# A graph-attention kernel on one core: the opening loads chained by waits instead of issued together

## The reference

```python
h = relu(layernorm(x))                      # x: 2048 x 256
type_sum = adj @ h                          # adj: 2048 x 2048 of 0 and 1, for both types
attn_a = sigmoid(concat([type_sum, h]) @ Wa.T + ba)
attn_b = sigmoid(concat([type_sum, h]) @ Wb.T + bb)
hw = h @ W_sa
scores = (hw @ a_left)[:, None] + (hw @ a_right)[None, :]
e = where(adj != 0, exp(-leaky_relu(scores, 0.01)), 0)
x_a = (e / (sum(e, axis=1) + 1e-5)) @ hw
x_b = adj @ (h @ W_gcnb) + b_gcnb
out = x + sigmoid(attn_a * x_a + attn_b * x_b)
```

## Time and profile before

| | |
|---|---|
| median of 3 runs | 190.69 us (190.56 to 190.69) |
| span of the profiled execution, first to last instruction | 189.2 us |
| total of the profiled execution | not given beside its span |
| TensorE matmul busy | 175.0 us, 92% |
| VectorE busy | 154.3 us, 82% |
| ScalarE busy | 117.3 us, 62% |
| GpSimd busy | 37.1 us, 20% |

### The profile page before, as it was taken

One profiled execution on the slowest core, in us unless ns is written; L12 is line 12 of the kernel. 1 busy time (PEld: TensorE's weight loads), 2 busy tenths in 40 slices (PEclk: granted clock), 3 DMA queues, 4 the chain that ended last, 5 costly groups with the idle time before them and its releaser, 6 DMA issues.

```text
span 189.2 us, 4431 instructions
## 1 busy us (share of the span) xinstructions
PE 175.0 (92%) x1576; PEld 144.4 (76%) x1576; DVE 154.3 (82%) x389; ACT 117.3 (62%) x231; POOL 37.1 (20%) x86
## 2 busy tenths in 40 slices
PE   0359899999999999999999999999999999999993
PEld 0335465466888888888888888888888888888892
DVE  0698789999999989996997898599869896997341
ACT  2197586899647958664696458466727764594310
POOL 1057770099970010002000200020020000000000
DMA  5920797000029008311901470175109210001100
GB/s 141 396 102 0 110 185 155 2 3 0 0 28 196 2 5 155 67 59 16 196 15 55 63 158 6 49 120 102 55 0 178 43 55 0 0 0 55 61 28 28
DMA packets 4621, 13.67 MB, mean 72 GB/s; under 512 B 512, under 2 KB 896, under 8 KB 4608
## 3 DMA queue, kind: packets, MB, share of 16 engines
q0 software_dynamic: 2304, 8.39, 24.8%
q1 hardware_dynamic: 2016, 4.20, 6.2%
q10 hardware_dynamic: 288, 0.92, 1.3%
HBM read 19.80 MB, written 2.10 MB: 116 GB/s over the span
## 4 chain that ended last, share of the span: by engine, by line
PE 80%; DVE 3%; issue 0%; ACT 0%; DVEq 0%
PE ps L800 15%; PE ps L801 15%; PE ps L807 14%; PE ps L808 14%; PE ps L806 14%; PE ps L765 4%; PE ps L838 1%; PE ps L837 1%; PE ps L836 1%; DVE mv_lo L603 1%; PE ps L756 1%; DVE h0t_lo L581 1%; DVE mv_lo L601 1%; PE ps L745 0%; DVE e_raw L342 0%; DVE far L333 0%
## 5 line engine op out<-in xcount | busy, mean ns | idle before, releaser
L349 ACT ACTIVATE e_raw<-e_raw,log_e 128x512 f32<-128x512 f32 x64 | 46.1, 720 | 43.9 <-DVE e_raw L342 43.1
L806 PE MATMUL ps<-mv_lo,e_hi 128*128 128x257 f16 x240 | 65.5, 273 | 0.0
L808 PE MATMUL ps<-mv_hi,e_lo 128*128 128x257 f16 x240 | 65.5, 273 | 0.0
L807 PE MATMUL ps<-mv_hi,e_hi 128*128 128x257 f16 x240 | 65.4, 272 | 0.0
L342 DVE SCALAR_TENSOR_TENSOR e_raw<-sl_row,exs,far 128x256 f32<-128x256 f16 (+1 forms) x128 | 56.6, 482 | 2.5 <-DVE far L333 2.0
L801 PE MATMUL ps<-mv_lo,adj 128*128 128x258 f16 x256 | 56.9, 272 | 0.0
L800 PE MATMUL ps<-mv_hi,adj 128*128 128x258 f16 x256 | 56.9, 273 | 0.0
L360 DVE TENSOR_TENSOR e_lo<-e_raw,e_hi 128x512 f16<-128x512 f32 x64 | 44.5, 697 | 3.8 <-ACT e_hi L356 3.8
L356 ACT ACTIVATE e_hi<-e_raw 128x512 f16<-128x512 f32 x64 | 39.3, 616 | 0.0
L800 PEld LDWEIGHTS ps<-mv_hi,adj 128*128 128x128 f16 x256 | 24.7, 96 | 3.8 <-ACT sl_row L471 0.2
L801 PEld LDWEIGHTS ps<-mv_lo,adj 128*128 128x128 f16 x256 | 24.8, 97 | 3.3
(11 more groups left out here) (80 smaller groups left out, 179.9 us busy)
## 6 DMA issues: line engine op xcount, KB each, us to landing
adj<-in_adj_t POOLq DMA_DIRECT2D x16, 512.0 KB, 7.1
x_sb<-in_x SPq DMA_DIRECT2D x4, 512.0 KB, 8.0
out<-res SPq DMA_DIRECT2D x7, 256.0 KB, 2.0
w_sb<-in_weights ACTq DMA_DIRECT2D x1, 512.0 KB, 8.1
c_sb<-in_consts ACTq DMA_DIRECT2D x1, 391.0 KB, 5.7
out<-res SPq DMA_DIRECT2D x1, 128.0 KB, 1.8
out<-res SPq DMA_DIRECT2D x2, 64.0 KB, 1.6
```

What stands on the lines that cost most here:

```text
L349: act.activation(e_raw[:, p % RING, :, :], e_raw[:, p % RING, :, :], ACT.Exp, bias=log_e[:, 0:1], scale=SLOPE - 1.0).then_inc(exp_done, 1)
L806: pe.matmul(a_bank(s, q), e_hi[:, j, cols], mv_lo[:, j, 0, 0:D + 1], start=(j == 0), stop=False)
L807: pe.matmul(a_bank(s, q), e_hi[:, j, cols], mv_hi[:, j, 0, 0:D + 1], start=False, stop=False)
L808: return pe.matmul(a_bank(s, q), e_lo[:, j, cols], mv_hi[:, j, 0, 0:D + 1], start=False, stop=(j == NT - 1))
```

## The change

SyncE now waits, before it issues each group of x but the first, until the group before has landed. ScalarE waits, before it issues consts and weights, until group 0 of x has landed. Nothing else is changed.

```diff
--- before.py
+++ after.py
@@ -228,6 +228,8 @@
         @block.sync
         def _(sp):
             for g in range(NG):
+                if g:
+                    sp.wait_ge(x_landed[g - 1], 16)
                 sp.dma_start(x_sb[:, g * GT:(g + 1) * GT, :], x[:, g * GT:(g + 1) * GT, :]).then_inc(x_landed[g], 16)
             with sp.Fori(0, NCH // 2 - 1) as r:
                 for s in range(2):
@@ -433,6 +435,7 @@
 
         @block.scalar
         def _(act):
+            act.wait_ge(x_landed[0], 16)
             act.dma_start(c_sb[:, :], consts).then_inc(c_landed, 16)
             act.dma_start(w_sb[:, :, :, :], weights).then_inc(w_landed, 16)
```

## The result

The kernel after takes 192.97 us (median of 4 runs, 192.81 to 193.21) against 190.69 us: ratio 1.0118, 95% interval 1.0106 to 1.0131, 2.28 us more. The forecast of 191.1 with a range up to 192.4 was wrong: the sign held, the size did not. The profiled execution took 192.81 us, with a span of 191.1 (before 189.2); the other three spans are 191.2 to 191.5, so it is the shortest of the four, and 1.9 us of the difference can be followed in it.

The account below looks back on a forecast made before the run. The prediction took the opening, up to the start of TensorE's adjacency and attention products, as the bound. Late consts move `relu_high(0)` from 12.03 to 12.5; 190.69 + 0.47 = 191.16, given as 191.1 us, range 190.0 to 192.4.

Parts of the forecast that it names:

- R: Start of `relu_high(0)` on ScalarE, 12.03 us before the change; forecast to move to 12.5 us.
- E: Start of the first `exs` on VectorE, 16.45 us before; forecast to move by 0.47 us, to 16.9.
- the idle spell before L451: Sign on ScalarE: idle time before this line, released by TensorE, the line starting at about 12.5 us.
- R = C + 3.9: Opening: `relu_high(0)` starts 3.9 us after consts land, behind `wl` and `turn(0)` on TensorE; 12.5 us forecast.
- Time = 190.69 + (C - 8.13): Kernel time for each rival, from the consts' landing time; a landing at 8.13 us is break-even.
- Part 2: Opening loads: consts issued behind group 0 at 4.56 land at 8.6 us instead of 6.56, the added cost.
- first touch of a new region: Opening of an adjacency load: the slow start isn't only sharing; first touch cost about 1 us there.
- Slower by much: Rival, opening loads: every fresh start is slow, consts again take 5.7 us; 192.8, half way 191.9; chance 0.13.
- No change: Rival, opening loads: x packets slow only from sharing, consts land between 7.75 and 8.5; centre 190.7 us; chance 0.25.
- Faster: Rival, opening loads: group 0 at full rate, consts land below 7.75; 189.9 us, at the middle 190.2; chance 0.15.
- The early transposes get quicker: Rival, TensorE's opening: gapless work speeds `turn(1)`, 190.8 us, or `turn(0)` itself, 190.3; chance 0.12.
- Parts 1 and 3: Opening loads: group 0 lands at 4.5 us, 1.85 earlier, table load hidden; weights and groups 1 to 3 hidden.

## Why the prediction went wrong

**The path was right.** What bounds the kernel, the fixed piece from R to E, TensorE taking over from ScalarE at R, the idle spell before L451 (now L454), `wl` and turn without a gap: all are in the profile after. R = C + 3.9 gives 14.0 for the measured C of 10.14, and R was 13.90; from R to E it was 4.44 us (4.42 before). Time = 190.69 + (C - 8.13) gives 192.7 for that C, and 192.97 was measured. Across the versions R, E and the time go together as long as group 1 of x is in time: R 11.19 with 189.90, 12.69 with 191.69, 13.04 with 191.87, 13.19 with 192.26, 13.90 with 192.97. The medians scatter about this by up to 0.4 us (with only ScalarE's wait R was 14.06 and the time 192.77); the spans don't: from E to the end of the span it was 172.7 to 172.8 us in all twelve profiled executions, the kernel before included. So nothing behind E took part in any of these differences.

**The step that failed is the sum for C** (C is the landing of the consts), in Part 2: "Consts land at C = 4.56 + 1.0 + 2.5 + 0.55 = 8.6 us." It was 10.14. Of the 1.54 us, about 0.4 is group 0's landing (4.97, not 4.5) and 1.1 the consts' own stage (5.2, not 4.05).

In the second, the failing term is the 2.5 us for "consts and group 1, interleaved": with the start of 1.0 and the tail of 0.55 left as they are, 3.6 were needed. It assumed that two queues that start together share the engines from the first packet and at full pace. ScalarE's queue gets next to nothing in its first microsecond beside SyncE's. The record had a sign of it that the prediction used only for a rival: before the change, too, consts were issued with group 0 at 0.86 and took 5.7 us, against 3.1 alone.

The prediction's reading that "c's packets took 163 ns from the first, so the slowness was x's" is wrong as well. The 163 ns are a mean over 5 us. In the first microsecond of data of the kernel before, ScalarE's queue showed, from 2.0 to 2.5 and from 2.5 to 3.0 us:

```profile
q10 hardware_dynamic: 5, 0.02, 22.4%
...
q10 hardware_dynamic: 5, 0.02, 10.8%
```

That is a mean of 266 ns for the consts' first ten packets (16.6% of 16 us), and in the next microsecond 157 (34 for 33.3%); SyncE's queue moved 32 packets meanwhile, then 36. Consts alone took 276 ns per packet in their first microsecond (45 for 77.6%). So the slow packets belong to the start and not to x, and the stage behind a wait pays for them again. Why they are slow no run shows, nor does any show the "first touch of a new region" to which the prediction put it down.

In the first, the data of group 0 alone took less per packet than I charged (193 ns, 38.6% of 64 us from 1 to 5 us for 128), but didn't end together. The windows from 2.5 to 4.5 us (engines' busy time, PEclk, DMA share, GB/s):

```profile
2.50:3.00 0.50, 0.00 (x0) 0.00 (x0) 0.00 (x0) 0.00 (x0) 0.00 (x0) 1.00 1.08 319
3.00:3.50 0.50, 0.00 (x0) 0.00 (x0) 0.00 (x0) 0.00 (x0) 0.00 (x0) 1.00 0.62 246
3.50:4.00 0.50, 0.00 (x0) 0.00 (x0) 0.00 (x0) 0.00 (x0) 0.00 (x0) 1.00 0.46 188
4.00:4.50 0.50, 0.00 (x0) 0.00 (x0) 0.00 (x0) 0.00 (x0) 0.00 (x0) 1.00 0.16 66
```

The engines are full for one half microsecond, and then their mean share falls to 0.62, 0.46 and 0.16 until the landing. The profile doesn't name single engines, but it shows 16 packets under 512 B, which I take for the ends of the load on the 16 engines (argued, not shown). Counted in half microseconds from 3.0 us on, they are 4, 6, 5 and 1. A mean per packet times 128 over 16 is too short for a load that ends so unevenly; 4.1 us for 512 KB alone is the right row.

**The rivals.** "Slower by much" is what happened, with a chance of 0.13: C = 10.2, 192.8. Its number was right partly by luck, as 4.5 + 5.7 has group 0 0.5 us too early and the stage 0.5 us too long. Its reason was half right: not every fresh start costs 5.7 us (consts alone took 3.1), but each start of consts on ScalarE's queue beside a load on SyncE's took 5.2 to 5.7. "No change" is out with C at 10.14. "Faster", by full-rate opening loads, is out: group 0 alone took 4.1 us. "The early transposes get quicker" is out too: `turn(0)`, directly behind `wl`, took 1.95 us for eight (2.08 before) and `turn(1)` 2.16 (2.17 before), far from the later 1.04. The granted clock reads 1.00, the level of 2.4 GHz, in every window of the opening, both where TensorE is slow and where it is fast, so this reading doesn't tell the two paces apart. Rather the slow pace lasted longer: the first products of `wide(0, 0)` took 0.63 us each up to 20.67, where before they took 0.38 from 17.39 on. It cost nothing, as E and the chain behind it don't wait for them: from E to the first adjacency product it was 28.54 us, before 28.49.

The Trainium skill's sum (DMA: Bandwidth & Descriptors, Anatomy of one DMA), which the page fits to transfers issued by GpSimd, gives as estimates 2.0 + 0.9 = 2.9 us for the consts alone, 2.0 + 1.2 = 3.2 for group 0 alone, and 4.1 for consts and group 1 together. Measured were 3.1, 4.1 and 5.2: near for the consts alone, short for the others.

**Parts 1 and 3.** The table load was hidden, as said, and the weights and later groups too: `w_hi` starts directly behind the `wx` copy. Group 1's load landed at 9.9, not 8.4, and its moments and guesses ended at 12.45, still ahead of the 13.4 at which the prediction had `norm(1)`; the slack of 2.5 us was 1.0. With only SyncE's waits, R at 11.63 and group 1 at 10.4, it became the limit and cost 0.6 us. That the chain of x loads is free was thus true of the full change and not by itself.

**What stays open.** Why ScalarE's queue starts behind SyncE's isn't shown, only that it does when both have a load; nor why the first packets of a start are slow.

## What to carry to other kernels

To have loads arrive in an order, put them in that order on one queue; a wait for the landing of one before the issue of the next adds the start and tail of a transfer (here 3.1 us for 391 KB alone that cost 1.0 us right behind another load), and it costs time where an engine has nothing else to do meanwhile. Before delaying a load, look for who waits for it first in each engine's list, and what stands behind that wait: here 3.8 us of TensorE work that had been free. And price a load by the row of a whole one like it, with what was issued beside it, not by packets.

## What the runs showed of the hardware

Of two loads issued at the same moment on SyncE's and ScalarE's queues, SyncE's was served first: 39 to 7 packets in the first microsecond of data, 49 to 8 with the contents swapped (issued at 5.00 and 5.01 us), 47 to 8 with consts against weights; at the start of the kernel before it was weaker, 32 to 10. Alone, ScalarE's queue moved 45. With SyncE's queue already filled with x, consts issued at 5.12 had two packets through by 8.0. The Trainium skill (DMA: Bandwidth & Descriptors, Queues, rings and completion order) says that each engine takes turns between the queues that have work. The profile's packet counts in the full change fit that in the third microsecond (49 and 56) and not in the first.

The first packets behind a start were slow whatever the load: 276 ns for consts alone and 240 for group 1 beside them in the first microsecond of data, against at most 160 for x at full rate. A load of 512 KB alone took 4.1 us, where one of 391 KB took 3.1 and a 256 KB store 2.0.
